# A four-layer graph network on one core: the last layer's first pass takes its destination rows from one-hot products

## The reference

```python
msg_s = (s_n @ Ws_src)[src] + (s_n @ Ws_dst)[dst]
msg_v = einsum(v_n, Wv_src)[src] + einsum(v_n, Wv_dst)[dst]
m1_s, m1_v = _cg_tp(msg_s, msg_v, y0, y1, *split(rbf @ W_rbf))   # product of 64 scalars, 32 vectors
a      = sum(leaky(m1_s @ W_alpha) * alpha_dot)                   # 4 scores per edge
val_s  = m1_s @ Ws_val;  val_v = einsum(m1_v, Wv_val)
val_v  = val_v * sigmoid(val_s @ Wg);  val_s = sigmoid(val_s)
m2_s, m2_v = _cg_tp(val_s, val_v, y0, y1, *w2)
h      = concat(m2_s @ Ws_vlin, einsum(m2_v, Wv_vlin))
out    = node + (segment sums over dst of softmax(a) * h) @ Wp
```

## Time and profile before

| | |
|---|---|
| median of 3 timed runs | 7612.11 us (7605.38 to 7612.97) |
| span of the profiled execution | 7980.6 us |
| first pass of layer 3 in it | 4588.9 to 7407.0 us |
| busy in the span | TensorE 88%, VectorE 82%, ScalarE 46%, POOL 67% |
| mean granted TensorE clock | 0.904 |

### The profile page before, as it was taken

How to read it: one execution, slowest core, us unless ns; L and a number is a source line. 1 busy time by engine, 2 the same in 40 slices (tenths; PEclk the granted TensorE clock), 3 DMA queues, 4 the chain that set the end, 5 groups by cost and what they waited for, 6 DMA issues and landing times. The chain is left out here.

```text
span 7980.6 us, 110610 instructions
## 1 busy us (share of the span) xinstructions
PE 7037.4 (88%) x32406; PEld 4813.5 (60%) x32406; DVE 6580.0 (82%) x18417; ACT 3693.0 (46%) x9602; POOL 5364.8 (67%) x4078
## 2 busy tenths in 40 slices
PE   6999999997999999899999788888888888888488
PEld 3444444444555555555555477777787777777366
DVE  7999999996788888688888677777787777777785
ACT  2444444443333333433333355555555555555385
POOL 1777777773577777377777188888888888887000
PEclk7999999996899999799999778888888888888698
DMA  7999999998222222122222133322222222222263
GB/s 211 167 168 170 167 169 165 166 162 189 52 65 66 66 65 61 37 68 69 69 69 69 32 68 76 73 68 71 73 76 69 74 70 72 72 72 71 68 192 107
DMA packets 459687, 776.87 MB, mean 97 GB/s; under 512 B 96721, under 2 KB 310966, under 8 KB 458838
## 3 DMA queue, kind: packets, MB, share of 16 engines
q0 software_dynamic: 274944, 469.50, 32.1%
q1 hardware_dynamic: 180038, 299.69, 12.3%
q10 hardware_dynamic: 4112, 0.62, 0.1%
HBM read 464.60 MB, written 304.85 MB: 96 GB/s over the span
## 5 line engine op out<-in xcount | busy, mean ns | idle before, releaser
L1446 DVE TENSOR_TENSOR work<-work 128x256 f32<-128x256 f32 (+5 forms) x5726 | 2483.9, 472 | 70.3 <-DMA work<-src_sum 27.6
L624 POOL DMA_INDIRECT fore<-node_table,src_i x1664 | 1709.7, 1027 | 655.9 <-issue 504.4
L662 POOL DMA_INDIRECT src_sum<-work,put_i x832 | 1325.2, 1593 | 557.1 <-ACT work L836 384.6
L624 POOL DMA_INDIRECT fore<-src_table,src_i x784 | 1218.3, 1554 | 406.8 <-issue 238.6
L624 POOL DMA_INDIRECT fore<-dst_table,dst_i x784 | 1090.0, 1390 | 238.9 <-issue 238.9
L1233 PE MATMUL bank<-work 128*128 128x384 f32 (+1 forms) x3328 | 1198.8, 503 | 10.4 <-DVE work L1446 10.4
L1330 PE MATMUL bank<-ident,work 128*128 128x128 f32 x4704 | 733.5, 297 | 444.4 <-DVE work L1446 444.4
L1233 PEld LDWEIGHTS bank<-work 128*128 128x128 f32 x3328 | 603.2, 191 | 688.2 <-issue 313.6
L1446 DVE TENSOR_TENSOR work<-work,bank 128x384 f32 (+6 forms) x2080 | 908.0, 437 | 78.4 <-issue 70.7
L1330 PEld LDWEIGHTS bank<-ident,work 128*128 128x128 f32 x4704 | 572.3, 151 | 566.7 <-DVE work L1446 506.0
L848 ACT ACTIVATE work<-bank 64x512 f32<-64x512 f32 x416 | 245.8, 591 | 1436.6 <-PE bank L1200 1436.6
(11 more groups left out here) (246 smaller groups left out, 13200.5 us busy)
## 6 DMA issues: line engine op xcount, KB each, us to landing
edge_h<-work SPq DMA_DIRECT2D x196, 320.0 KB, 2.3
work<-edge_h SPq DMA_DIRECT2D x196, 320.0 KB, 3.4
work<-keys SPq DMA_DIRECT2D x196, 256.0 KB, 5.8
fore<-node_table,src_i POOLq DMA_INDIRECT x1664, 2.7
work<-in_edge_attr SPq DMA_DIRECT2D x196, 128.0 KB, 5.9
src_sum<-work SPq DMA_DIRECT2D x4, 6240.0 KB, 37.5
work<-src_sum SPq DMA_DIRECT2D x100, 240.0 KB, 4.3
src_sum<-work,put_i POOLq DMA_INDIRECT x832, 5.9
```

The source lines that it names most:

```text
L624: return pool.indirect_dma_start(dst, None, table, bass.IndirectOffsetOnAxis(ap=idx, axis=0), bounds_check=bound, oob_is_err=True)
L662: pool.indirect_dma_start(src_sum[t], bass.IndirectOffsetOnAxis(ap=put_i[:, e:e + 1], axis=0), E.run[:, g % 2, t * 480:(t + 1) * 480], Non ...
L1446: return V_.tensor_tensor(o, p, q, op)
```

## The change

The source tables and the destination rows of the last layer's first pass are obtained differently:

- **Destination rows** are no longer gathered. SP loads the group's keys (`dst_keys`), VectorE compares them (`turned`, four comparisons, three groups ahead), TensorE multiplies by the window's 160 columns, which lie in `skip` (`dst_rows`, five halves ahead, into banks 4 and 5), and `m1` adds the gathered source row and this product from PSUM.
- **Banks**: since banks 4 and 5 now hold those rows (one copy, four tiles), `turn_m2` uses banks 1 and 2, as `turn_m1` does, with waits between the two.
- **Border rows**: an edge of a border tile whose destination is in the next window gets no product. For the 24 border tiles the sums of source and destination rows are made beforehand: 24 gathers, 24 gathers that add, one store behind `src_table`'s end; the index of such an edge (`put_i`) points there. The indices are computed by small VectorE steps, one for each group from group 8 of layer 1 on (`border_tiles`).
- The maps (`values`, `linear`) are left as they are.

```diff
@@ SP, before the pass and in it
+                for g in range(2):
+                    dst_keys(g)
+                    rbf(g)
+                sp.wait_ge(s.border_rows, 16 * MORE)
+                sp.dma_start(src_table[ROWS:ROWS + MORE * P].rearrange("(k p) c -> p k c", p=P), T.border).then_inc(s.border_kept, 16)
+                unrolled(GROUPS, [(0, lambda g: rbf(g) if g >= 2 else None), (-2, lambda g: dst_keys(g) if g >= 2 else None), (5, keep_h)])
@@ POOL
+                for k in range(MORE):
+                    gather(T.border[:, k, :], src_table[0:ROWS], border_src_i[:, k:k + 1], last_row).then_inc(s.border_src_in, 16)
+                pool.wait_ge(s.border_src_in, 16 * MORE)
+                for k in range(MORE):
+                    pool.indirect_dma_start(T.border[:, k, :], None, dst_table, bass.IndirectOffsetOnAxis(ap=border_dst_i[:, k:k + 1], axis=0),
+                                            compute_op=ALU.add, bounds_check=last_row, oob_is_err=True).then_inc(s.border_rows, 16)
+                pool.wait_ge(s.border_kept, 16)
...
-                        gather(T.gs[:, b, t, :], src_table, src_i[:, e:e + 1], last_row).then_inc(
+                        gather(T.gs[:, b, t, :], src_table, put_i[:, e:e + 1], last_src_row).then_inc(
                             got[3][b], 16)
-                        gather(T.gd[:, b, t, :], dst_table, dst_i[:, e:e + 1], last_row).then_inc(
-                            got[3][b], 16)
@@ ScalarE, m2_turned
-                    act.activation(T.t2[:, h % 2], bank[:, 4:6, 0:384], ACT.Copy).then_inc(s.m2_in_sbuf, 1)
+                    act.activation(T.t2[:, h % 2], bank[:, 1:3, 0:384], ACT.Copy).then_inc(s.m2_in_sbuf, 1)
@@ TensorE, turn_m1
+                    if h >= 4:
+                        pe.wait_ge(s.m2_in_sbuf, h - 3)
+                    elif h:
+                        pe.wait_ge(s.m1_in_sbuf, h)
                     turn3(T.f, h, 1, s.m1_turned)
+
+                def dst_rows(h):
+                    g, at = h // 2, h % 2 * 2
+                    if h % 8 == 0:
+                        n = min(16, TILES - 2 * h)
+                        pe.load(held[0:n], tile_window_i[0:1, 2 * h:2 * h + n])
+                    if at == 0:
+                        pe.wait_ge(s.dst_turned, g + 1)
+                        if g:
+                            pe.wait_ge(s.rows_added, g)
+                    for t in range(2):
+                        window = pe.snap(held[(2 * h + t) % 16], min_val=0, max_val=WINDOWS - 1)
+                        last = nc.tensor.matmul(gd[:, at + t, 0:DIM], T.turned[:, g % 2, at + t, :],
+                                                skip[:, bass.ds(window, 1), 0:DIM].rearrange("p o c -> p (o c)"),
+                                                start=True, stop=True)
+                    last.then_inc(s.dst_rows_mm, 1)
@@ TensorE, turn_m2 and the loop
-                    turn3(T.f2, h, 4, s.m2_turned)
+                    pe.wait_ge(s.m1_in_sbuf, min(h + 4, TILES // 2))
+                    if h > TILES // 2 - 4:
+                        pe.wait_ge(s.m2_in_sbuf, h)
+                    turn3(T.f2, h, 1, s.m2_turned)
-                unrolled(TILES // 2, [(-3, turn_m1), (1, linear), (-3, values), (0, turn_m2), (-6, edge_w3)])
+                unrolled(TILES // 2, [(-3, turn_m1), (1, linear), (-3, values), (-5, dst_rows), (0, turn_m2), (-6, edge_w3)])
@@ VectorE, m1 and the loop
-                    dve.wait_ge(got[3][depth], (g // DEPTH + 1) * (16 * 2 * GROUP))
-                    tt(m, T.gs[:, depth], T.gd[:, depth], ALU.add).then_inc(s.rows_added, 1)
+                    dve.wait_ge(got[3][depth], (g // DEPTH + 1) * (16 * GROUP))
+                    dve.wait_ge(s.dst_rows_mm, 2 * g + 2)
+                    tt(m, T.gs[:, depth], gd[:, :, 0:DIM], ALU.add).then_inc(s.rows_added, 1)
...
+                def turned(g):
+                    b = g % 2
+                    dve.wait_ge(s.dst_keys_in1 if b else s.dst_keys_in0, 16 * (g // 2 + 1))
+                    if g >= 2:
+                        dve.wait_ge(s.dst_rows_mm, 2 * g - 2)
+                    for t in range(GROUP):
+                        e = g * GROUP + t
+                        last = V_.tensor_scalar(T.turned[:, b, t, :], T.keys[:, b, t, :], src_f[:, e:e + 1], None, ALU.is_equal)
+                    last.then_inc(s.dst_turned, 1)
-                unrolled(GROUPS, [(-1, m1), (0, m2), (2, edge_out)])
+                unrolled(GROUPS, [(-1, m1), (0, m2), (-3, turned), (2, edge_out)])
@@ VectorE, border_tiles: one step for each group of layer 1 from group 8 on, cut to its core
+                for k in range(MORE):
+                    done()
+                    V_.scalar_tensor_tensor(B.lower, B.window, float(k + 1), B.one, ALU.is_lt, ALU.mult,
+                                            accum_out=B.before[:, k:k + 1]).then_inc(dve_own, c.step())
+                    yield
...
+                    V_.tensor_copy(border_src_i[:, k:k + 1], src_i[:, bass.ds(at, 1)]).then_inc(dve_own, c.step())
+                    V_.tensor_copy(border_dst_i[:, k:k + 1], dst_i[:, bass.ds(at, 1)]).then_inc(dve_own, c.step())
+                    yield
```

More of the change, by code:

```diff
@@ L238, in build @@
             "h_done", "h_kept0", "h_kept1",
+            "tiles_in", "border_src_in", "border_rows", "border_kept", "dst_keys_in0", "dst_keys_in1", "dst_turned", "dst_rows_mm",
             "scores_turned", "scores_in_sbuf", "scan_ready", "scan_turned", "scan_free", "scores_shifted")}
@@ L319, in l3_views @@
             v.rb = g(2, 512)
[L320 to L321 removed]
+            v.gs = fore[:, 0:2560].rearrange("p (b t c) -> p b t c", b=DEPTH, c=DIM)
+            v.keys = fore[:, 2560:3584].bitcast(I32).rearrange("p (b t n) -> p b t n", b=2, n=P)
+            v.turned = fore[:, 3584:4608].rearrange("p (b t n) -> p b t n", b=2, n=P)
             v.m = g(GROUP, DIM)
@@ L324, in l3_views @@
             v.cv = g(2, GROUP, 196)
+            at_f = g.used()
             v.f, v.f2 = g(2, GROUP, 352), g(2, GROUP, 352)
+            v.border = work[:, at_f:at_f + MORE * DIM].rearrange("p (k c) -> p k c", c=DIM)
             v.t1, v.t2 = g(2, 2, 384), g(2, 2, 384)
@@ L337, in build, with border_views, get @@
         T = l3_views()
+        def border_views():
+            flat = aux[:].rearrange("p t c -> p (t c)")
+            at = [0]
+            def get(n):
+                at[0] += n
+                assert at[0] <= ALL_TILES * 5
+                return flat[:, at[0] - n:at[0]]
+            v = type("Border", (), {})
+            v.firstI, v.window, v.one, v.lower, v.src = get(TILES).bitcast(I32), get(TILES), get(TILES), get(TILES), get(TILES)
+            v.before, v.none, v.shift, v.dst, v.inside, v.mask, v.rest, v.row = (get(MORE) for _ in range(8))
+            v.tile_i = get(MORE).bitcast(I32)
+            return v
+        B = border_views()
         def pass2_views():
@@ L405, in rows_mm, with dst_rows_mm @@
             return bank[:, 2 + 2 * k:4 + 2 * k, :].rearrange("p b (t c) -> p (b t) c", c=256)
+        def dst_rows_mm():
+            return bank[:, 4:6, :].rearrange("p b (t c) -> p (b t) c", c=256)
         def conv_view(l):
@@ L1499, in _ @@
             V_.tensor_scalar(U.lane, spare[:], 1.0, -float(ROWS), ALU.mult, ALU.add).then_inc(dve_own, c.step())
+            V_.tensor_scalar(lane[:], spare[:], 1.0, -float(ROWS), ALU.mult, ALU.add).then_inc(dve_own, c.step())
             big = Nv.big.rearrange("p (j c) -> p j c", c=DIM)
@@ L1802, in _, with border_tiles, done @@
             windows = [None] * 32
+            own_tiles = [dve.alloc_register(f"dve_tile{i}") for i in range(8)]
+            def border_tiles():
+                def done():
+                    dve.wait_ge(dve_own, c.n)
+                dve.wait_ge(s.tiles_in, 16)
+                V_.tensor_scalar(tile_window_i[:], B.firstI, 7, 31, ALU.logical_shift_right, ALU.bitwise_and).then_inc(dve_own, c.step())
+                V_.memset(B.one, 1.0).then_inc(dve_own, c.step())
+                yield
+                done()
+                V_.tensor_copy(B.window, tile_window_i[:]).then_inc(dve_own, c.step())
+                yield
+                done()
+                V_.tensor_scalar(src_f[:, 0:TILES], B.window, float(P), lane[:], ALU.mult, ALU.add).then_inc(dve_own, c.step())
+                yield
+                for k in range(MORE):
+                    done()
+                    V_.scalar_tensor_tensor(B.lower, B.window, float(k + 1), B.one, ALU.is_lt, ALU.mult,
+                                            accum_out=B.before[:, k:k + 1]).then_inc(dve_own, c.step())
+                    yield
+                done()
+                V_.tensor_copy(B.src, src_i[:, 0:TILES]).then_inc(dve_own, c.step())
+                V_.tensor_scalar(B.none, B.before, 0.5, 8192.0, ALU.is_lt, ALU.mult).then_inc(dve_own, c.step())
+                yield
+                done()
```

(47 more changed lines are left out.)

25 lines of the change are left out of this document (20 added, 5 removed).

## The result

The changed kernel takes 8639.8 us (median of 4, 8635.5 to 8642.9) against 7608.7 us: a ratio of **1.135, 95% interval 1.133 to 1.137**, 1031 us slower. The forecast was 8484 us, slower, by a ring of waits. One execution of the kernel before in the second session (9049.0 us at clock 0.764) ran in a slower state than all others and is left out of the ratios of that session.

The account below looks back on a forecast made before the run. POOL's gathers were taken to bound the last layer's first pass. Pass +782, ahead of it +82, layer 1 +8 gave +872 on the 7980.6 us span: 8853, less the 368.5 gap to the median, 8484 us; range 8050 to 8720.

Parts of the forecast that it names:

- The ring: Last layer's first pass: m1 waits for TensorE's dst_rows, turn_m1 waits for m1, once per group; forecast's chance 0.74.
- Its length at full clock: One turn through turn_m1, linear, values, dst_rows and m1 in the pass: 15.87 us a group before any clock loss.
- The clock: TensorE's granted clock falls after each idle wait in the pass: 2.5 us a group lost, ends 0 and 3.25.
- The new idle is nearest to the long one: TensorE's new 3.4 us idle was likened to today's 3.15 us idle, after which 3.25 us of work is lost.
- The pass: Last layer's first pass, 196 groups at 18.37 us: 3600 us, +782.
- Ahead of the pass: Border gathers, adding gathers, landings and table write before the first group: +82 us, from 60 to 105.
- Layer 1: Small VectorE steps for border indices, slipped into groups 8 on: +8 us, 0 to 30.
- POOL, the keys and the comparisons: In the pass, POOL has ample room, key loads are landed in time, comparisons run beside TensorE: no cost.
- If the gap stays, 8484: The profiled span exceeds the timed median by 368.5 us; taking that as unchanged turns span 8853 into 8484 us.
- The third reading: The gap is a 0.09 us cost of each POOL operation, making the first pass 142 us shorter untraced: 8626 us.
- The range: Whole kernel 8050 to 8720 us, from 0.3 us a group clock loss to 3.25 with the gather gap reading.
- The faster rival: In the pass, m1 isn't late behind dst_rows; about 12.5 us a group, 7334 us in all; chance 0.11.

Follow-up runs that it names:

- Runs 1 and 3: Run 1: changed kernel with dst_rows six halves ahead instead of five, 7586.9 us. Run 3: changed kernel plus 24 idle transposes before turn_m1's wait, 8268.2 us.
- run 12: Changed kernel with dst_rows ahead of values, still five halves ahead, plus 12 idle transposes in TensorE's wait: 8056.1 us on a third chip (kernel before 7605.6).
- Run 2: Changed kernel with dst_rows ahead of values in TensorE's list, still five halves ahead: 8625.3 us.
- run 4: Kernel before with destination-row gathers left out from group 4 on, four gathers a group, output not the reference's: 7381.3 us against 7604.2, ratio 0.969.

## Why the prediction was right, and where its sizes were off

**The ring** was right: its place, its direction and its one turn a group. Runs 1 and 3 show it, run 12 measures a piece of it. The time of 8639.8 us lies in the range, but the last part below shows that this was in part luck.

**Its length at full clock**, 15.87 us, was 15.03. The mis-sized term is `dst_rows`: 0.92 us a half with a pause of 0.28 taken from layer 0, and 0.54 us measured (5997.74 to 5998.28), without a pause. In the ring it stands twice, which makes 0.76 of the 0.84. The window's number comes from a register here too, so the register alone doesn't make the pause of layer 0; what makes it no run shows.

**The clock**, 2.5 us a group, was 1.9 (16.91 against 15.03). The clock was 0.84 in the pass, and the turns looked at have stretches near half clock. The Trainium skill's rule ("TensorE: Matmul & The Clock Gate", HAM oscillation), that a wait in each trip drops the clock, agrees with this trace (0.57 and 0.60 behind the two waits). That each trip begins slow, as the prediction put it, doesn't hold for the turn at 6020.96. And the step "The new idle is nearest to the long one" took the loss to grow with the idle time. Run 2 has 2.1 us idle and loses 2.9; the changed kernel has 3.6 and loses 1.9. The rows say where the difference lies: what counts is how much of the half-clock time falls under work, nearly all of it in run 2's turn, only a part in the changed kernel's.

**The pass**: +782 foreseen, +560 in the traces. The two terms above are 280 us too much (0.84 + 0.6 us by 196 groups); some 60 the other way are what the sum left out, since it took the pass to be 196 turns and nothing more: from its beginning to the first store of h the changed kernel needs 165 us, of which 81 are the border work and 17 one group. **Ahead of the pass**: +82 foreseen, 81 measured; the additions took 1.55 us each, 1.86 from start to start, within the bound from the scatter, 44 us in all and not 38. **Layer 1**: +8 foreseen; the pass begins 10 us later, which can't be told from none (see run 4's 17 above). **POOL, the keys and the comparisons** cost nothing in the ring, as said; once it is open the comparisons do: 11.61 against run 4's 10.97 us, and they (busy 0.87 us a group) are the one kind of operation that VectorE has there and not in run 4.

**From the span to the median** the sum failed. "If the gap stays, 8484" took the 368.5 us as constant. As far as the differences show (run 4 above all), it belonged to one stage of one execution, and went with it: 872 foreseen for the span, 653 measured; 872 for the median, 1031 measured. The step that failed is reading the trace's 14.38 us a group as this kernel's usual time. An over-long ring (219 us too much) and an over-long pass before (378 us too little) partly cancelled, which is luck: with the second put right and the first as it was, the forecast would have been 8859 us, above the range. The third reading, a cost hidden in the POOL-bound pass, had the right stage, at 142 us instead of about 378. Its cause, a cost of each of POOL's operations that only the trace has, is out: in the changed kernel, with 3342 of them, the traced execution is as fast as the others. The range itself was summed short: by its own terms (3.25 us of clock, 142 us of gap) its upper end is 8773 and not 8720.

**The faster rival** would have needed the ring under 12.5 us. Its sum of what the engines need alone was near the truth (11.61 measured once the order allowed it), and even so the change would have been worth 0.3%: 82 us ahead of the pass against 100 or so in it.

## What to carry to other kernels

A new wait must be followed both ways: list what the waited-for engine has to do, in its own fixed order, between the signal and the next thing that it needs back, and compare that with the other engine's time for it; here 1.7 us against 5.0 made a ring that, with the clock it cost, took 1053 us, and an offset of one in a software pipeline removed it. Two engines that wait for each other as often as the loop runs, neither full, are the sign of it. And before a stage's time from one trace is taken as the kernel's, set the trace's span beside the timed runs: a gap of 5% belongs to some stage, here, as far as differences can tell, to the one whose gathers are slowed by another engine's work. And a clock loss isn't read from the length of the idle time alone, but from the time at half clock that falls under work.

## What the runs showed of the hardware

- Useless transposes made the kernel 372 us faster (8639.8 to 8268.2), with the granted clock in the pass at 1.00 and not 0.84.
- In these two orders the clock's loss didn't grow with the idle time: 2.1 us idle a turn cost 2.9 us, 3.6 us cost 1.9 us. In the first, 5.8 us of work ran at 0.50; in the second, stretches of 5.3 and 4.2 us had 0.57 and 0.60.
- The same kernel before took 7604, 7606 and 8270 us on three chips, one session on each, with 387 us of the difference in layers 1 and 2 at a granted clock of 0.90 against 0.99; whether that is the chip or the session isn't shown. Ratios between kernels differ too (border work beside the groups: 0.958 and 0.987).
- A gather beside m1 of VectorE takes up to 3.73 us, bare 1.01, on both the first and the second chip; with six or four gathers a group VectorE is 99% busy, so this costs the pass nothing.
